# Probabilities brought back in one transfer, cut into high and low parts 1024 elements at a time, and the inverse row sums turned as one 32x32 block

## The reference, cut to what matters

```python
q = split_heads(h @ Wq.T + bq); k = ...; v = ...
scores = jnp.einsum('bhqd,bhkd->bhqk', q, k) * scale
scores = jnp.where(mask, -jnp.inf, scores)
attn = jax.nn.softmax(scores, axis=-1)
out = jnp.einsum('bhqk,bhkd->bhqd', attn, v)
out = out.transpose(0, 2, 1, 3).reshape(b, n, D_MODEL)
return out @ Wo.T + bo      # then x = layernorm(x + ...)
```

## Time and profile before

| what | us |
|---|---|
| runs, median (lowest to highest) | 3178.0 (3174.58 to 3180.0), 3 runs |
| span of the profiled execution | 3177.6 |
| TensorE busy, matmuls | 2986.1 (94%) |
| VectorE busy | 2630.0 (83%) |
| ScalarE busy | 2481.0 (78%) |
| GpSimd busy | 2079.3 (65%) |

### The profile page before, as it was taken

One profiled execution on the slowest core, in us unless ns is written; L12 is line 12 of the kernel. 1 busy time (PEld: TensorE's weight loads), 2 busy tenths in 40 slices (PEclk: granted clock), 3 DMA queues, 4 the chain that ended last, 5 costly groups with the idle time before them and its releaser, 6 DMA issues.

```text
span 3177.6 us, 60582 instructions
## 1 busy us (share of the span) xinstructions
PE 2986.1 (94%) x19084; PEld 2513.6 (79%) x19084; DVE 2630.0 (83%) x6553; ACT 2481.0 (78%) x5543; POOL 2079.3 (65%) x1927
## 2 busy tenths in 40 slices
PE   5899999999999999999999999999999999999995
PEld 4788888887888887788887887887888877888874
DVE  4788888888888888888888888888888888888874
ACT  3778788777788877888778887777888877888764
POOL 1566676666766666766667766666766666766664
PEclk7999999999999999999999999999999999999997
DMA  3677887777877777887777787777777778877765
GB/s 123 193 220 220 222 230 221 212 218 208 232 231 222 216 218 205 232 230 219 215 215 218 225 235 207 214 212 221 224 228 223 212 216 223 228 221 223 206 198 148
DMA packets 290047, 681.92 MB, mean 215 GB/s; under 512 B 40512, under 2 KB 74048, under 8 KB 256960
## 3 DMA queue, kind: packets, MB, share of 16 engines
q1 hardware_dynamic: 289728, 678.05, 75.0%
HBM read 375.40 MB, written 302.51 MB: 213 GB/s over the span
## 4 chain that ended last, share of the span: by engine, by line
PE 42%; DMA 25%; POOL 9%; DVE 8%; ACT 8%; SPq 3%; issue 3%; ACTq 0%; DVEq 0%; POOLq 0%
PE R_bank L724 27%; DMA turned_lo_prob<-scratch 12%; DMA scratch<-blocked 9%; PE O_bank L813 8%; POOL turned_lo_prob L1163 7%; PE S_bank L794 5%; DVE blocked L1105 3%; DMA r_wide<-r_scratch 3%; ACT turned_hi_prob L841 3%; SPq L628 3%; PE L_bank L715 2%; ACT prob L927 2%; POOL o_half L1158 1%; DVE qk_pair L1002 1%; ACT o_half L946 1%
## 5 line engine op out<-in xcount | busy, mean ns | idle before, releaser
L1163 POOL TENSOR_TENSOR turned_lo_prob<-turned_lo_prob,turned_hi_prob 128x512 fp32r<-128x512 f32 x1024 | 1297.1, 1297 | 564.0 <-ACT turned_hi_prob L841 563.2
L927 ACT ACTIVATE prob<-prob,small_cols 128x512 f32<-128x512 f32 x1024 | 729.8, 714 | 152.2 <-DVE small_cols L1085 143.9
L841 ACT ACTIVATE turned_hi_prob<-turned_lo_prob 128x512 fp32r<-128x512 f32 x1024 | 596.6, 622 | 228.1 <-DMA turned_lo_prob<-scratch 218.4
L1105 DVE STREAM_TRANSPOSE blocked<-prob 128x512 f32<-128x512 f32 x1024 | 692.4, 695 | 76.3 <-ACT prob L927 40.3
L1085 DVE CUSTOM_DVE_ANT_0 prob<-S_bank,mask 128x512 f32<-128x512 f32 x1024 | 677.2, 680 | 24.1 <-PE S_bank L794 20.1
L813 PE MATMUL O_bank<-turned_hi_prob,v_st 128*128 128x256 f32 x2048 | 528.2, 294 | 86.9 <-POOL turned_lo_prob L1163 83.6
L813 PE MATMUL O_bank<-turned_lo_prob,v_st 128*128 128x256 f32 x2048 | 513.6, 287 | 0.0
L813 PEld LDWEIGHTS O_bank<-turned_hi_prob,v_st 128*128 128x128 f32 x2048 | 398.3, 195 | 136.8 <-POOL turned_lo_prob L1163 125.3
L794 PE MATMUL S_bank<-qk_pair 64*128 64x512 f32 x3072 | 445.6, 416 | 16.3 <-DVE small_cols L1085 9.3
L724 PE MATMUL R_bank<-wv,x1T 128*128 128x256 f32 x3072 | 401.3, 286 | 1.6 <-DVE v_st L984 1.5
L813 PEld LDWEIGHTS O_bank<-turned_lo_prob,v_st 128*128 128x128 f32 x2048 | 399.6, 195 | 3.4
(11 more groups left out here) (90 smaller groups left out, 4390.0 us busy)
## 6 DMA issues: line engine op xcount, KB each, us to landing
scratch<-blocked SPq DMA_DIRECT2D x256, 1024.0 KB, 4.6
turned_lo_prob<-scratch SPq DMA_DIRECT2D x1024, 256.0 KB, 5.5
tokens<-xT SPq DMA_DIRECT2D x128, 256.0 KB, 4.8
tokens<-x SPq DMA_DIRECT2D x128, 256.0 KB, 3.8
r_wide<-r_scratch SPq DMA_DIRECT2D x512, 64.0 KB, 3.4
out<-tokens SPq DMA_DIRECT2D x128, 256.0 KB, 4.0
r_scratch<-r_cols SPq DMA_DIRECT2D x256, 2.0 KB
tokens<-adj SPq DMA_DIRECT2D x1, 1024.0 KB, 6.5
```

The source lines that it names most:

```text
L841: act.activation(dst, src, ACT.Copy).then_inc(done, 1)
L927: act.activation(prob_tile(R, s), prob_tile(R, s), ACT.Exp, bias=negmax[:, slot:slot + 1], scale=-1.0, accum_out=psum_row[:, ph % 2, j:j + ...
L1105: dve.transpose(blocked[:, ph % 2, :, :, 2 * (s % 2) + s % 4 // 2, :].rearrange("p d c i -> p c d i"), prob_tile(R, s).rearrange("p (c d i ...
L1163: pool.tensor_tensor(turned_lo_prob[:, ph % 2, a, :, :], turned_lo_prob[:, ph % 2, a, :, :].bitcast(F32), turned_hi_prob[:, a, :, :].bitca ...
```

## The change

Five things are edited together.

1. The four transfers of `load_probs` become one of 1 MB over 128 partitions, on one semaphore for each half of the double buffer. For this partition p must hold key 4i+d of a chunk where it held key 32d+i. So `turn_blocks` reads the tile with a step of four elements, `(c i d)` in place of `(c d i)`; what it writes is laid out as before.
2. `probs_hi` and `probs_lo` take 1024 elements per partition: 16 of each to a round instead of 32.
3. `r_cols` is 128x32. The four reciprocals stand next to each other, and one 32x32 block per group of partitions is turned.
4. `store_sums` stores all 128 rows of 32 elements (128 B each), 16 KB where it was 2 KB; only 4 of 32 rows of each group hold sums. `load_sums` reads what it read.
5. The plans have half as many `hi` and `lo`. Most often the first of two neighbours stays in its place and the other is dropped. All other steps keep their order.

```diff
-UNITS = {... "hi": (32, 0), "lo": (32, 0), ...}
+UNITS = {... "hi": (16, 0), "lo": (16, 0), ...}
-        scratch = nc.dram_tensor("scratch", [4, P, 4 * N], F32, kind="Internal").ap()
-        r_scratch = nc.dram_tensor("r_scratch", [4, 4, 4, BLK], F32, kind="Internal").ap()
+        scratch = nc.dram_tensor("scratch", [4, 4, P, N], F32, kind="Internal").ap()
+        r_scratch = nc.dram_tensor("r_scratch", [4, BLK, 4, BLK], F32, kind="Internal").ap()
-        r_cols = sb("r_cols", [P, 4, BLK])
+        r_cols = sb("r_cols", [P, BLK])
...
             def store_probs(R, ph):
...
-                sp.dma_start(scratch[ph % 4, :, :],
+                sp.dma_start(scratch[ph % 4, :, :, :].rearrange("a (j d) x -> (a j) (d x)", d=4),
                              blocked[:, ph % 2, :, :, :, :].rearrange("p d c j i -> p (d c j i)")).then_inc(p_stored[ph % 2], 16)
             def load_probs(R, ph):
                 sp.wait_ge(*stored(R, ph))
-                by_key_block = scratch[ph % 4, :, :].rearrange("(a j) (d x) -> d j a x", a=4, d=4)
-                for d in range(4):
-                    sp.dma_start(turned_lo_prob[BLK * d:BLK * (d + 1), ph % 2, :, :, :].rearrange("p a c x -> p a (c x)").bitcast(F32),
-                                 by_key_block[d]).then_inc(moved(R, ph, d)[0], 16)
+                sp.dma_start(turned_lo_prob[:, ph % 2, :, :, :].rearrange("p a c x -> p a (c x)").bitcast(F32),
+                             scratch[ph % 4, :, :, :].rearrange("a p x -> p a x")).then_inc(moved(R, ph)[0], 16)
             def store_sums(R, ph):
...
                 sp.dma_start(r_scratch[ph % 4, :, :, :].rearrange("j a i -> a j i"),
-                             r_cols[0:P:BLK, :, :]).then_inc(r_stored, 16)
+                             r_cols[:, :]).then_inc(r_stored, 16)
...
             def weigh(R, g):
-                pe.wait_ge(p_lo, R.n(32, 4 * ph + 4))
+                pe.wait_ge(p_lo, R.n(16, 2 * ph + 2))
...
             def probs_hi(R, m):
-                ph, a = m // 4, m % 4
+                ph, a = m // 2, m % 2
...
-                split_hi(turned_hi_prob[:, a, :, :], turned_lo_prob[:, ph % 2, a, :, :].bitcast(F32), p_hi)
+                split_hi(turned_hi_prob[:, 2 * a:2 * a + 2, :, :], turned_lo_prob[:, ph % 2, 2 * a:2 * a + 2, :, :].bitcast(F32),
+                         p_hi)
...
             def invert_sums(R, ph):
-                dve.reciprocal(r_cols[:, :, 0], psum_row[:, ph % 2, :]).then_inc(p_inv, 1)
+                dve.reciprocal(r_cols[:, 0:4], psum_row[:, ph % 2, :]).then_inc(p_inv, 1)
                 dve.wait_ge(p_inv, R.n(8, ph + 1))
-                dve.transpose(r_cols[:, :, :], r_cols[:, :, :]).then_inc(r_turned, 1)
+                dve.transpose(r_cols[:, :], r_cols[:, :]).then_inc(r_turned, 1)
...
             def turn_blocks(R, s):
                 dve.transpose(blocked[:, ph % 2, :, :, 2 * (s % 2) + s % 4 // 2, :].rearrange("p d c i -> p c d i"),
-                              prob_tile(R, s).rearrange("p (c d i) -> p c d i", c=T, i=BLK)).then_inc(p_turned, 1)
+                              prob_tile(R, s).rearrange("p (c i d) -> p c d i", c=T, i=BLK)).then_inc(p_turned, 1)
...
             def probs_lo(R, m):
-                ph, a = m // 4, m % 4
-                pool.wait_ge(p_hi, R.n(32, m + 1))
-                pool.tensor_tensor(turned_lo_prob[:, ph % 2, a, :, :], turned_lo_prob[:, ph % 2, a, :, :].bitcast(F32),
-                                   turned_hi_prob[:, a, :, :].bitcast(F32), ALU.subtract).then_inc(p_lo, 1)
+                ph, a = m // 2, m % 2
+                pool.wait_ge(p_hi, R.n(16, m + 1))
+                lo_ap = turned_lo_prob[:, ph % 2, 2 * a:2 * a + 2, :, :]
+                pool.tensor_tensor(lo_ap, lo_ap.bitcast(F32), turned_hi_prob[:, 2 * a:2 * a + 2, :, :].bitcast(F32),
+                                   ALU.subtract).then_inc(p_lo, 1)
```

More of the change, by code:

```diff
@@ L82 @@
     "exp pre1 hi C0",
[L83 to L86, removed]
+    "hi exp exp",
+    "exp exp aexp1",
+    "lows hi pre2",
+    "hi exp exp",
     "exp evQ2 aexp2 fin0",
     "C1 turn fin1 hi",
-    "fin2 hi exp pre3",
-    "C2 evW0 hi hi",
+    "fin2 exp pre3",
+    "C2 evW0 hi",
     "evW1 aexp3 lows evW2",
     "exp exp exp evW3",
-    "C3 turn hi hi",
-    "hi exp hi A0",
+    "C3 turn hi",
+    "hi exp A0",
     "lows exp fin3 exp",
@@ L97 @@
     "lap2 E0 turn hi",
-    "E1 hi lows hi",
-    "hi E2 lap3 exp",
+    "E1 lows hi",
+    "E2 lap3 exp",
     "E3 exp exp turn",
     "exp evV0 evV1 A1",
-    "hi hi hi B0",
-    "exp lows hi exp",
+    "hi hi B0",
+    "exp lows exp",
     "exp exp evQ4 turn",
-    "lows A2 hi hi",
+    "lows A2 hi",
     "B1 hi evV2 exp",
-    "evV3 hi exp exp",
+    "evV3 exp exp",
     "A3 turn B2 exp",
-    "exp lows hi hi",
-    "hi hi turn B3",
+    "exp lows hi",
+    "hi turn B3",
     "exp",
@@ L148 @@
     "norm turn",
[L149 to L152, removed]
+    "lo",
+    "lo",
+    "lo",
+    "lo",
     "yrs norm",
-    "lo lo",
+    "lo",
     "turn lo",
-    "lo norm",
+    "norm",
     "turn lo",
-    "lo lo",
-    "lo lrs",
+    "lo",
+    "lrs",
     "A0 norm",
     "bo0 turn",
-    "lo lo",
-    "lo lo",
+    "lo",
+    "lo",
     "norm turn",
     "A1 lo",
-    "lo lo",
-    "lo norm",
+    "lo",
+    "norm",
     "turn bo1",
     "A2 lo",
-    "lo lo",
-    "lo norm",
+    "lo",
+    "norm",
     "A3 turn",
     "norm lo",
-    "lo lo",
-    "lo turn",
+    "lo",
+    "turn",
     "bo2 bo3",
@@ L219 @@
     "evQ1 exp exp lows turn",
-    "exp hi hi hi exp",
-    "hi exp exp exp hi",
-    "hi hi lows hi exp",
+    "exp hi hi exp",
+    "exp exp exp hi",
+    "hi lows exp",
     "exp turn evQ2 exp hi",
-    "hi hi hi evW0 lows",
+    "hi evW0 lows",
     "evW1 exp exp exp exp",
     "turn evW2 lows evW3 hi",
-    "hi exp hi exp hi",
+    "exp hi exp",
     "evQ3 exp exp turn hi",
-    "hi hi hi exp exp",
+    "hi exp exp",
     "exp lows fin0 exp exp",
[L231 to L235, removed]
+    "fin1 turn fin2 hi",
+    "hi lows exp exp",
+    "exp hi hi turn",
+    "fin3 lows turn hi",
+    "hi lows turn",
 )
@@ L257 @@
     "norm turn lo",
[L258 to L272, removed]
+    "lo",
+    "lo lo",
+    "norm turn",
+    "lo lo",
+    "norm turn",
+    "lo lo",
+    "norm yrs",
+    "turn lo",
+    "lo norm",
+    "turn lo",
+    "lo norm",
+    "lo turn",
+    "lo norm",
+    "turn lo",
+    "lo norm",
     "turn",
@@ L494, in graph_layers @@
         bias_hi, bias_lo, bias_mm, bias_done = sem("bias_hi"), sem("bias_lo"), sem("bias_mm"), sem("bias_done")
-        p_moved = [[sem(f"p_moved{i}{a}") for a in range(4)] for i in range(2)]
+        p_moved = [sem(f"p_moved{i}") for i in range(2)]
         p_stored = [sem(f"p_stored{i}") for i in range(2)]
@@ L934, in probs_hi @@
                 if a == 0:
[L935 to L937 removed]
+                    act.wait_ge(*moved(R, ph))
+                split_hi(turned_hi_prob[:, 2 * a:2 * a + 2, :, :], turned_lo_prob[:, ph % 2, 2 * a:2 * a + 2, :, :].bitcast(F32),
+                         p_hi)
             def half_lows(R, u):
```

12 lines of the change are left out of this document (5 added, 7 removed).

## The result

The changed kernel takes 3224.6 us (median, 3218.2 to 3226.8), the kernel before, timed beside it, 3176.3. The ratio is 1.0144, 95% interval 1.0124 to 1.0163: 46 us slower by the ratio (48 by the two medians). The forecast was slower too, but 3345 us, with 3270 to 3430 as its own range. The time is that of the rival "half a column time", 3225 to 3240 us.

The account below looks back on a forecast made before the run. VectorE was to replace TensorE as bound: 97.7 us work, 0.4 for the store and 3.3 idle make 101.4 us a round, 5.4 more; times 31 that is 167, so 3177.6 + 167 = 3345 us, range 3270 to 3430.

Parts of the forecast that it names:

- half a column time: Rival on the 32 strided turns: 8.2 us a round more, VectorE at 89.6 us, time 3225 to 3240 us; chance 0.22.
- the bound: Steady round: VectorE's work grows from 82.2 to 97.7 us, so it replaces TensorE (busy 92.75 of 96 us) as bound.
- the price of the step: Strided read in the 32 block transposes: one more column time per column, 0.51 us each, 16.3 us a round.
- the single load: Load of probabilities: lands 1.6 us earlier, but nothing put into the sum, since VectorE will not be waiting for it.
- splits, sums and store: Per round: splits of 1024 zero, smaller turn of inverse sums -0.8 us, longer store of sums +0.4 us.
- the free-step rival: Strided turns cost nothing, TensorE stays the bound, sooner probabilities give 3147 us; chance 0.22, of which 0.17 faster.
- the cap of 3.25 us a round: TensorE's idle time in a steady round, the most the single load could give back were TensorE still the bound.
- Coarser splits at zero: Splits of 1024: 3.1 us a round saved on ScalarE and on GpSimd, but counted zero, hidden behind VectorE.
- The wide store: Store of sums: four DMA engines, 28 more pieces each, 1.7 us more per store, 0.4 us a round put in.
- The DMA rival: Store of sums fills four DMA engines, 29.5 us a round more on each, 104.4 us a round, 3438 us; chance 0.08.
- The estimate from the Trainium skill's page "Vector Engine (DVE) Microarchitecture Reference": Strided read of the block transposes: 0.35 to 0.74 us more each, 11 to 24 us a round.

## Why the prediction was right in its sign and wrong in its size

The direction and the bound were right. Two terms of the sum were mis-sized: the price of the step, taken at one column time, and the single load, put at zero. What each is worth depends on the order in which the parts are laid together:

| us | forecast | step first | load first |
|---|---|---|---|
| the step | +180 | +101 | +139 |
| one load for four | 0 | -41 | -79 |
| splits, sums and store | -12 | -14 | -14 |
| all | +167 | +46 | +46 |

The forecast's +180 is (82.2 + 16.3 + 3.3 - 96) x 31, its -12 is -0.4 x 31. The measured columns are differences of ratios. In either order one of the two terms is off by 79 us and the other by 41.

- *The bound.* Right: VectorE took over, and its 52% of the chain, 8% before, says so.
- *The price of the step* is the first step that failed. It was put at 0.51 us and is 0.40. No row gave a value; one column time was chosen between two distant rows. This is 3.4 us a round: with 0.40 the same sum is 94.3 + 3.7 = 98.0 us a round and 3240 us, so that it carries 105 of the 121 us between forecast and time. The table has less for the step, 41 to 79 us off, because there VectorE's longer idle time counts with it. VectorE's work is 91.02 x 97.3/96 = 92.3 us, not 94.3. Most of these 2 us can be read: the round of the earlier trace rows was a full one (over 24 rounds it is 81.6 us in 96, not 82.2), and instructions that overlap count once; the groups' times exceed VectorE's busy time by 312 us before and 346 after, 1.1 a round more. VectorE idles 5.0 us a round, where 3.7 was put in.
- *One load for four* is the second. It was forecast at zero, "since VectorE will not be waiting for it", and is worth 41 us where VectorE is 91% busy and 79 us where it is not. The reasoning took busy time for a wall. VectorE's idle time consists largely of waits for ScalarE, and a later load holds ScalarE's queue with all that stands behind it, such as layer 0's `h`. The row with 218.4 us of ScalarE waits had it, and I let VectorE's load cover it. The gain of the free-step rival had the same fault, 31 us forecast and 79 measured: the cap of 3.25 us a round was taken, and then a third of it. In fact TensorE's wait for low parts fell by 88 us over the span.
- *The time of the rival with half a column time came true*, though the step is dearer than its 0.26 us. That the sum with the right price (3240 us) comes so near is in part luck: the load's gain, VectorE's smaller work and its longer idle time nearly cancel.
- *Coarser splits at zero*: right within 10 us beside one load, wrong with four (19 us). The cover was the sooner landing, not VectorE: from 0.9751 to 0.9741 they and the sums are even with a VectorE that is second.
- *The wide store*: the engines and packets were exact; 0.4 us a round was its price. Beside four loads it costs 22 us, beside one nothing that was measured.
- *The DMA rival* didn't come: the share fell.
- *The estimate from the Trainium skill's page "Vector Engine (DVE) Microarchitecture Reference"*, 0.35 to 0.74 us for the step, held the measured 0.40 near its lower end. The sum's 0.51 lay inside it too.

## What to carry to other kernels

Cost each part against the kernel that the other parts leave, not against the kernel before: here the same splits and the same sums cost 42 us beside four loads, and beside one they lie between 14 us gained and 10 lost. In this loop with a fixed order on every engine, a transfer that lands sooner paid even where another engine was over 90% busy; read what the waiting engine has queued behind the wait. If a reordering needs a wide step, divide it into steps of two words, or put it where few elements pass: evacuating k takes 8 instructions a round, turning probabilities 32. Then look at who else reads what was reordered: here it was layer 0's mask.

## What the runs showed of the hardware

- A VectorE block transpose of 128x512 f32 reads with a step of one or two words, or in pairs with a hop of 32 words, in 0.70 us; with a step of 4 words in 1.10 and of 16 words in 1.07 us.
- Reading PSUM with a step of four words costs neither VectorE (742 ns, contiguous 741) nor ScalarE (686 ns both ways) anything.
- A bf16 mask as second source of a 128x512 reduction on VectorE, read in turn from four quarters of a row, takes 1552 ns against 1067 contiguous; in turn from two halves 1066.
- One transfer of 1 MB over 128 partitions takes 61 to 64% of the DMA engines' time in this kernel, four of 256 KB over 32 partitions 73 to 76%. The median from issue to landing is 5.6 to 5.7 us for the one, and 4.9 to 5.6 us for each of the four (6.3 where `r_wide` came in twice the pieces).
- 128 rows of 128 B stored on four DMA engines, 256 times, cost 22 us beside four loads.
- In the kernel where `r_wide` lands 1.9 us later (5.3 in place of 3.4 us) the time is 160 us longer; the probabilities land later there too (6.3 in place of 5.5 us).
